# A transformer block on one core: row sums of a head scaled and inverted once for four tiles, four transposing transfers per head, and key preparation placed behind the inverse

## The reference

```python
x = x + top_k_mask(softmax(x) * s * t / sqrt(512), k=5120)   # diagonal left out
x1 = ln(x) * (1 + scale1) + shift1
q, k, v = split(x1 @ qkv_w + qkv_b)
attn = softmax(q @ k.T * 128**-0.5)
x = x + gate1 * (attn @ v @ out_w + out_b)
x2 = ln(x) * (1 + scale2) + shift2
x = x + gate2 * (gelu(x2 @ ffn_w1 + ffn_b1) @ ffn_w2 + ffn_b2)
```

## Time and profile before

| What | us |
|---|---|
| three runs, lowest / median / highest | 1552.26 / 1552.96 / 1553.39 |
| the profiled execution | 1553.78 |
| its span, first to last instruction | 1551.9 |
| PE busy in it | 1500.0 |
| DVE busy | 1117.5 |
| ACT busy | 885.0 |
| POOL busy | 408.0 |

### The profile page before, as it was taken

How to read it: one execution, slowest core, us unless ns; L and a number is a source line. 1 busy time by engine, 2 the same in 40 slices (tenths; PEclk the granted TensorE clock), 3 DMA queues, 4 the chain that set the end, 5 groups by cost and what they waited for, 6 DMA issues and landing times.

```text
span 1551.9 us, 21298 instructions
## 1 busy us (share of the span) xinstructions
PE 1500.0 (97%) x7157; PEld 1245.9 (80%) x7157; DVE 1117.5 (72%) x2424; ACT 885.0 (57%) x1631; POOL 408.0 (26%) x243
## 2 busy tenths in 40 slices
PE   1999899999999999999999999999999999999998
PEld 1877788778888888888878888888878888888987
DVE  7878888876796887776785887776786666664431
ACT  4556677764855666662753666763572655654340
POOL 6713545554120322220000322221000122222000
PEclk9999999999999999999999999999999999999999
DMA  7866799987666677775464877687464786786463
GB/s 292 303 260 188 223 214 270 246 230 283 244 239 233 168 211 202 202 203 190 166 227 184 231 187 211 154 211 217 163 231 181 199 217 152 202 207 161 183 237 119
DMA packets 334508, 327.58 MB, mean 211 GB/s; under 512 B 270752, under 2 KB 275008, under 8 KB 331328
## 3 DMA queue, kind: packets, MB, share of 16 engines
q1 hardware_dynamic: 334112, 325.90, 69.9%
q10 hardware_dynamic: 288, 0.33, 0.1%
HBM read 204.54 MB, written 54.54 MB: 167 GB/s over the span
## 4 chain that ended last, share of the span: by engine, by line
PE 88%; DVE 6%; ACT 2%; DVEq 2%; issue 1%; DMA 1%; SPq 0%; ACTq 0%
PE bank L1390 27%; PE bank L1392 26%; PE bank L1391 26%; PE bank L1712 2%; PE bank L1610 1%; PE bank L1605 1%; DVEq L1216 1%; PE bank L1606 1%; DVE tb L1029 1%; PE bank L1422 1%; ACT halves L892 1%; DVE halves L1233 1%; PE bank L1444 1%; PE bank L1441 1%; PE bank L1440 1%
## 5 line engine op out<-in xcount | busy, mean ns | idle before, releaser
L742 POOL CAST probT<-turned 128x2048 fp32r<-128x2048 f16 x128 | 243.3, 1914 | 699.2 <-DMA turned<-halves 399.6
L1390 PE MATMUL bank<-xT,w 128*128 128x512 f32 x704 | 279.7, 397 | 0.0
L1391 PE MATMUL bank<-xT,w 128*128 128x512 f32 x704 | 273.9, 389 | 0.0
L1392 PE MATMUL bank<-xT,w 128*128 128x512 f32 x704 | 273.8, 389 | 0.0
L885 ACT ACTIVATE prob<-bank,nbias 128x512 f32<-128x512 f32 x256 | 176.4, 690 | 113.1 <-DVE nbias L1217 104.1
L1233 DVE SCALAR_TENSOR_TENSOR halves<-prob,rinv,halves 128x512 f16<-128x512 f32 x256 | 175.4, 748 | 25.7 <-ACT halves L892 25.0
L892 ACT ACTIVATE halves<-prob,rinv 128x512 f16<-128x512 f32 x256 | 164.5, 713 | 32.9 <-DVE rinv L1229 32.9
L1215 DVE TENSOR_REDUCE rowmax<-bank 128x1 f32<-128x512 f32 x256 | 174.4, 681 | 0.3 <-issue 0.3
L1392 PEld LDWEIGHTS bank<-xT,w 128*128 128x128 f32 x704 | 132.1, 188 | 28.0
L1390 PEld LDWEIGHTS bank<-xT,w 128*128 128x128 f32 x704 | 132.9, 189 | 25.0
L1391 PEld LDWEIGHTS bank<-xT,w 128*128 128x128 f32 x704 | 132.4, 188 | 24.9
(11 more groups left out here) (171 smaller groups left out, 3328.8 us busy)
## 6 DMA issues: line engine op xcount, KB each, us to landing
w<-split_weights SPq DMA_DIRECT2D x154, 1024.0 KB, 5.8
split_weights<-w SPq DMA_DIRECT2D x38, 1024.0 KB, 6.6
wraw<-weights_in SPq DMA_DIRECT2D x48, 512.0 KB, 4.8
split_weights<-xT SPq DMA_DIRECT2D x7, 1024.0 KB, 7.6
adaw<-ada_w_in SPq DMA_DIRECT2D x4, 1536.0 KB, 13.1
xr<-x_in SPq DMA_DIRECT2D x4, 1024.0 KB, 6.3
split_weights<-qk SPq DMA_DIRECT2D x3, 1024.0 KB, 7.7
adj<-x_in SPq DMA_DIRECT2D x3, 1024.0 KB, 9.2
```

What stands on the lines that cost most here:

```text
L742: nc.gpsimd.tensor_copy(probT[:, :, :, rows].rearrange("p a j (i t) -> p i (a j) t", i=2), turned_of(h)[:, 2 * pair:2 * pair + 2, :, :]).t ...
L1390: pe.matmul(dst, w_hi_ap, x_hi_ap, start=first, stop=False)
L1391: pe.matmul(dst, w_hi_ap, x_lo_ap, start=False, stop=False)
L1392: return pe.matmul(dst, w_lo_ap, x_hi_ap, start=False, stop=last)
```

## The change

Six things are edited, and nothing is computed otherwise except that row sums are scaled and inverted for four tiles at once.

- turn: four transfers of one tile each, in place of two of two tiles; each has a semaphore (turned_in[0] to [3]) and waits for one tile of the low halves.
- widen: four casts of one tile, 128 x 1024, in place of two of 128 x 2048.
- head on DVE: one wait for all four exps, one scale and one reciprocal over four columns, in place of a pair of each over two. V_DOWN has the value of 1 / P_UP.
- In heads 1 to 4 of sequence 0 this stands ahead of the key preparation, which stood ahead of it.
- topk_adj writes its reciprocal into factor in place of rinv, which now holds values still in use.
- The scaling of s (scale_s) moves from head 0 to head 1 of each sequence.

```diff
@@ turn (SP)
-                for pair in range(PAIRS):
+                for i in range(NT):
                     if k:
-                        wait_apart(sp, widened, (k - 1) * PAIRS + pair + 1)
-                    wait_apart(sp, p16_lo, k * NT + 2 * (pair + 1))
-                    sp.dma_start_transpose(
-                        turned_of(h)[:, 2 * pair:2 * pair + 2, :, :].rearrange("p i n t -> p (i n) t"),
-                        halves_of(h)[:, 2 * pair:2 * pair + 2, :, :].rearrange("p i a s -> p (i a s)"))\
-                        .then_inc(turned_in[pair], 16)
+                        wait_apart(sp, widened, (k - 1) * NT + i + 1)
+                    wait_apart(sp, p16_lo, k * NT + i + 1)
+                    sp.dma_start_transpose(turned_of(h)[:, i, :, :],
+                                           halves_of(h)[:, i, :, :].rearrange("p a s -> p (a s)"))\
+                        .then_inc(turned_in[i], 16)
@@ widen (POOL)
-                for pair in range(PAIRS):
-                    wait_apart(pool, turned_in[pair], 16 * (k + 1))
+                for i in range(NT):
+                    wait_apart(pool, turned_in[i], 16 * (k + 1))
                     pool.wait_ge(pv_done, b * H + h)
-                    rows = slice(2 * pair * P, 2 * (pair + 1) * P)
                     nc.gpsimd.tensor_copy(
-                        probT[:, :, :, rows].rearrange("p a j (i t) -> p i (a j) t", i=2),
-                        turned_of(h)[:, 2 * pair:2 * pair + 2, :, :]).then_inc(widened, 1)
+                        probT[:, :, :, i * P:(i + 1) * P].rearrange("p a j t -> p (a j) t"),
+                        turned_of(h)[:, i, :, :]).then_inc(widened, 1)
@@ head (ACT)
                 for i in range(NT):
-                    act_e.wait_ge(rinv_ready, k * PAIRS + i // 2 + 1)
+                    act_e.wait_ge(rinv_ready, k + 1)
@@ topk_adj (DVE)
-                V.reciprocal(rinv[:, lo:hi], nxsum[:, lo:hi])
+                V.reciprocal(factor[:, lo:hi], nxsum[:, lo:hi])
                 dve.drain()
-                V.tensor_tensor(factor[:, lo:hi], rinv[:, lo:hi], scur[:, lo:hi], ALU.mult)
+                V.tensor_tensor(factor[:, lo:hi], factor[:, lo:hi], scur[:, lo:hi], ALU.mult)
@@ topk_under_head (DVE)
                 elif h == 1:
+                    scale_s(t)
                     topk_adj(t, 0, 2)
@@ head (DVE)
+                dve.wait_ge(exp_done, b * (H * NT) + h * NT + NT)
+                V.tensor_scalar(rowsum[:, :], rowsum[:, :], V_DOWN, None, ALU.mult)
+                dve.drain()
+                V.reciprocal(rinv[:, :], rowsum[:, :]).then_inc(rinv_ready, 1)
                 keys_first = is_first(b) and 0 < h < FIRST_TOTAL
                 if keys_first:
                     topk_under_head(b + 1, h)
-                for pair in range(PAIRS):
-                    two = slice(2 * pair, 2 * pair + 2)
-                    dve.wait_ge(exp_done, b * (H * NT) + h * NT + 2 * pair + 2)
-                    V.tensor_scalar(rowsum[:, two], rowsum[:, two], 1.0 / P_UP, None, ALU.mult)
-                    dve.drain()
-                    V.reciprocal(rinv[:, two], rowsum[:, two]).then_inc(rinv_ready, 1)
@@ attend (PE)
-                pe.wait_ge(widened, (b * H + h + 1) * PAIRS)
+                pe.wait_ge(widened, (b * H + h + 1) * NT)
```

More of the change, by code:

```diff
@@ L362, in block_kernel @@
         rinv_ready, p16_hi, p16_lo = sem("rinv_ready"), sem("p16_hi"), sem("p16_lo")
-        turned_in, widened = [sem("turned_in0"), sem("turned_in1")], sem("widened")
+        turned_in, widened = [sem(f"turned_in{i}") for i in range(NT)], sem("widened")
         y_done, y_gated, y_back = sem("y_done"), sem("y_gated"), sem("y_back")
@@ L887, in head @@
                 if k:
-                    for pair in range(PAIRS):
-                        act_e.wait_ge(turned_in[pair], 16 * k)
+                    for i in range(NT):
+                        act_e.wait_ge(turned_in[i], 16 * k)
                 for i in range(NT):
-                    act_e.wait_ge(rinv_ready, k * PAIRS + i // 2 + 1)
+                    act_e.wait_ge(rinv_ready, k + 1)
                     nc.scalar.mul(halves_of(h)[:, i, 0, :], prob[:, i, :], rinv[:, i:i + 1]).then_inc(p16_hi, 1)
@@ L1049, in topk_rowmax, with scale_s @@
                         .then_inc(xmax_ready, 1)
-                dve.wait_ge(small_in, 16)
+            def scale_s(t):
                 src = small[:, COLS["s"][0]:COLS["s"][1]].rearrange("p (b i) -> p b i", b=B)
@@ L1362, in _ @@
             topk_rowmax(0)
+            dve.wait_ge(small_in, 16)
+            scale_s(0)
             topk_adj(0, 0, 2)
```

## The result

The changed kernel is slower: 1565.01 us, median of 4 runs (1564.05 to 1566.87), against 1552.61 for the kernel before, measured beside it (1550.46 to 1553.39). The ratio over these runs is 1.0085, 95% interval [1.007, 1.01] (the quotient of the two medians is 1.0080). The prediction was 1550.8, with a range of 1547.5 to 1554.0: the result lies 11 us above the range, on a side to which I had given 0.08. The profiled execution took 1566.87 us, its span 1564.9, at a granted clock of 0.993.

The account below looks back on a forecast made before the run. TensorE bounds the kernel; only its 8.5 us of waits in sequence 0 can be won. +3.0 (to head 5) - 0.4 - 0.5 + 1.2 - 1.1 = 2.2 us gained on 1552.96 gives 1550.8, range 1547.5 to 1554.0.

Parts of the forecast that it names:

- Nothing that the change saves or loses in the other 49 heads can be seen: After head 14 of sequence 0 PE never waits for attention, so savings there stay unseen; only 8.5 us can be won.
- the sum's 0.67: Single sum makes L1233 0.67 late; it shows in head 0 of sequences 1 to 3, loss 1.1 us.
- the stalls of L1059 and scur: DVE stalls under casts in sequence 0: 0.95 saved at L1059, 1.64 by moving scur to head 1, 0.1 paid.
- the term for head 3: PE's gap ahead of head 3 of sequence 0 was to fall from 1.23 to 0.30 us.
- rival C: Rival, 0.19: casts fall among the four L1233 of waiting heads, up to 1.04 each; two eat the gain: 1553.0.
- The swap by itself is worth nothing: Heads 1 to 4 of sequence 0: key work starts 1.29 later, L1233 follows at once; DVE is the chain either way.
- the 2.8 that I had credited to the swap: Gain of 2.8 us from smaller PE gaps ahead of heads 1 to 4 of sequence 0, as key work avoids casts.
- My net gain of 0.3: Head 4 of sequence 0: gap ahead of head 5 grows from 1.02 to 2.4, the weight half's 1.64 goes.
- A stand costs its length: Unwritten step in all sums: a standstill of PE costs only its own length.
- Price 0: Four transposes in place of two were taken to have no fixed price per transfer, ending about 0.6 us earlier.
- B: Rival, 0.08: fixed price per transfer on the queue, 2 us later at heads 3, 7 and 11 of sequence 0: 1556.8.
- the losses that I gave to the casts: Sequence 0: short casts delay the third weight split in heads 8 and 12, losing 0.4 ahead of head 9, 0.5 ahead of 13.

Follow-up runs that it names:

- one sum alone: Kernel before with only the row sums changed to one scale and one reciprocal over four tiles, behind the fourth exp: 1558.52 us, ratio 1.0035.
- pairs back: Changed kernel with its single sum of a head taken back to two pairs; reordering and four transfers stay: 1559.07 us, ratio 1.0043 to before.
- the short casts alone: Kernel before with only four transfers and four casts per head; row sums in pairs, order as before: 1550.67 us, ratio 0.9989.
- the changed kernel less its reordering: Changed kernel with the swap alone undone, key work first again in heads 1 to 4 of sequence 0: 1561.70 us, ratio 1.0051 to before.
- the one with the weight half held: Changed kernel; in heads 1 to 4 of sequence 0 GpSimd's weight half waits for VectorE's four low parts: 1562.54 us, ratio 1.006 to before.
- the one without long stands: Kernel before plus four transfers and casts, scale moved, sums (pairs) before keys in heads 1 to 3 of sequence 0, weight half held there: 1546.96 us, ratio 0.9965.

## Why the prediction was wrong, point by point

**"Nothing that the change saves or loses in the other 49 heads can be seen": this step failed first.** It rests on the earlier trace rows, the waits of PE, and these tell what PE waits for, not how near the next engine is. In heads 1 to 4 of sequences 1 and 2 DVE carries the key work too, and its round was as long as PE's 13.6 us already. The round is a closed chain of row maxima, exps, products, low halves, low parts, key work, v and output piece, and then the next head's row maxima. The first of these starts 1.59 us after the scores where the chain has caught up (from head 6 on), and 2.62, 2.41, 2.84, 2.40 and 2.24 in heads 1 to 5 of sequence 1 of the kernel before: it was behind. In the changed kernel it is 2.97, 2.27, 3.37, 4.62 and 5.08. I charged the sum's 0.67 to head 0 alone (0.25 ahead of head 1: that is what was measured in sequences 1, 2 and 3) and wrote that others hide it. Head 4 of sequence 1 of the changed kernel, on DVE and then two casts of POOL:

```profile
554.52 2.74 DVE L1231 SCALAR_TENSOR_TENSOR halves<-prob,rinv,halves 128x512 f16<-128x512 f32 x4 [0.87 <-ACT halves L890]
557.18 1.40 DVE L1185 SCALAR_TENSOR_TENSOR qk<-bank,small,qk 128x512 fp32r<-128x512 f32 x2
558.67 0.43 DVE L1071 TENSOR_SCALAR tb<-adj 128x512 int32<-128x512 int32 x1
559.18 1.37 DVE L1073 TENSOR_TENSOR adj<-adj,tb 128x512 int32<-128x512 int32 x1
...
562.50 0.69 DVE L1180 SCALAR_TENSOR_TENSOR v<-bank,v 128x512 fp32r<-128x512 f32 x1 [0.39 <-ACT v L867]
563.11 0.74 DVE L1185 SCALAR_TENSOR_TENSOR act<-bank,small,act 128x512 fp32r<-128x512 f32 x1
```
```profile
558.82 1.18 POOL L740 CAST probT<-turned 128x1024 fp32r<-128x1024 f16 x1 [9.29 <-DMA turned<-halves]
560.32 1.13 POOL L740 CAST probT<-turned 128x1024 fp32r<-128x1024 f16 x1 [0.32 <-DMA turned<-halves]
```

The key work slides under a cast and L1073 takes 1.37 (0.69 in the kernel before). The last row of DVE is the low part of the output, for which take_total behind the scores of head 5 waits, since both use bank 6: 563.85, and PE stood there since 561.5. Most of the 5.2 us that sequence 1 loses is paid at this one place, 2.39 us, and then 1.7 more of lower clock; 0.25 lies ahead of head 1 and 0.7 in head 4 (0.38 of it a wait for split weights). That the sum makes the round late is shown (one sum alone: 3.1 us per sequence; pairs back: none); how much of it is the 0.67 and how much the key work meeting casts is only read from these rows. The waits for split weights are a second way by which the late round reaches PE: 0.3 to 0.9 us in head 4 of sequences 1 and 2 in all five kernels with one sum in every head, and in sequence 1 of no kernel with pairs.

**The swap: gains right, collision missed.** I had the stalls of L1059 and scur gone and the gaps ahead of heads 1 to 4 at 0.24, 0.18, 0.30 and 0. They were 0.17, 0.54, 2.18 and 0. What failed is the term for head 3, by the mechanism of my rival C, but with the wrong partner: C had casts of at most 1.04 fall on L1233, and counted against itself that no L1233 had ever met a cast. What the swap brings there is the weight half, 2.4 to 2.6 us long, since it makes ACT's products, and with them its weight cast and POOL's subtraction, earlier by the length of the key work, while the low halves stay where they are. "The swap by itself is worth nothing" followed DVE alone and not what ACT and POOL would do sooner. Before that, the short casts alone had already taken 1.9 us off the waits ahead of heads 2 to 4 (1.55, 1.23 and 0.70 became 0.67, 0.94 and none): two thirds of the 2.8 that I had credited to the swap. The Trainium skill, page "SBUF — State Buffer" (Who interferes with whom), says that a DVE instruction with two SBUF inputs and a GpSimd instruction that reads SBUF get in each other's way, by an exclusive lock. The traces agree for the weight half, nearly in full: 2.74 became 4.88 beside a 2.48. They do not for L651, which ran beside the four of head 1 for 1.4 us and made them 0.48 longer. The page would have told me to look at every long POOL instruction, not at the casts alone.

**Head 4: right, with a price that I hadn't.** No wait ahead of head 4 and at the weight half, and 3.01 ahead of head 5 where I had 2.4; the exps ended 9.3 us after the scores' start instead of 8.85, and the scale and reciprocal, the key work and the four low halves follow them one after the other. My net gain of 0.3 was a loss of 0.4 for the stand and of 3.0 for the clock behind it.

**A stand costs its length: this step failed without being written down.** All sums took it so. It held for the kernel before, whose stands ended at 1.65. Of what the changed kernel lost, some 8 us are matmuls at the lower level (1.7 + 3.0 + 1.7 + 1.7), and only some 6 are longer stands; the earlier start of sequence 0 takes 1.1 off again.

**Four transfers: right in total, two terms not.** Price 0 or below (1.6 us faster, alone); SP stayed under 6 us for four, which rules out B. Casts 1.06. With four transfers alone the wait ahead of head 14 fell from 1.64 to 0.45, as forecast (0.4). But the losses that I gave to the casts ahead of head 9 (0.4) and head 13 (0.5) came to under 0.1 each there. In the changed kernel PE stands still for 0.56 ahead of head 9, and the single sum is needed for it: 0.57 in the changed kernel less its reordering, under 0.1 with the pairs back. Ahead of head 13 it is 0.88 (I had 1.2), ahead of head 14 none.

**The sum.** In place of +3.0 to head 5, -0.9 + 1.2 and -1.1 came: heads 0 to 5 of sequence 0 -4.1, its later heads +0.9, sequences 1 to 3 -11.1.

## What to carry to other kernels

A list of waits of the bounding engine shows who is late, not who is next; before counting a delay as hidden, measure for each stage how far the feeding engine's round is behind (here the first row maximum after the scores), since a round that is as long as the bounding one hides nothing and adds up its losses until a shared buffer makes them due. When work is moved on one engine, follow what the others then do earlier: a gain of 3 us on paper became a loss of 7.5 when the reordering was made alone, because a GpSimd instruction of 2.5 us slid onto VectorE's two-input operations and, in head 4, key work came behind late exps. With head 4 left as it was, one wait that keeps the two engines apart was worth 5.2 us. And a stand of TensorE of some 2 us and more should be priced with the matmuls behind it.

## What the runs showed of the hardware that I had not expected

- Stands of TensorE of up to 1.88 us were never followed by the lower clock (28 of them), those of 2.17 us and more mostly (18 of 23), for 1.4 to 3.0 us of loss each; equal stands at equal places went both ways. The times of kernels with such stands also vary more: 1559.09 to 1566.30 for the one with the weight half held, 1546.12 to 1548.17 for the one without long stands.
- Four SBUF-to-SBUF transposes of 128 x 1024 took no measurable time more than two of 128 x 2048 for the kernel: 5.55 against 4.98 us on the queue, and the first tile lands earlier.
- Where four low halves (2.74 us) met a weight half of 2.4 to 2.9 us they took 4.83 to 4.92, and 5.36 where they met the clearing of the diagonal (L651 or L652) as well. Beside that one alone they took 3.22, and 3.06 to 3.18 where some of them met a cast (head 5 of three kernels), so rival C's collision exists too, at 0.3 to 0.4 us.
